# Latent attention on one Trainium2 core: the order of its pieces from a list scheduler, and score maxima issued singly

## The chip, the core and the metric

The kernel runs on one core of one Trainium2 chip. The metric is the device time of one execution in microseconds (us). The kernel before was run three times: median 1757.98 us, lowest 1755.6, highest 1759.52. The five engines that matter are called here by the names of the profile: PE (TensorE), DVE (VectorE), ACT (ScalarE), POOL (GpSimd) and SP (SyncE, which issues DMAs).

## What is computed

The whole program is a stack of layers on one sequence of 2048 tokens of 128 numbers: a mixture of experts, a windowed attention, the mixture again, the latent block, a state space layer, and the latent block a second time. The change touches only the attention inside the latent block, so it acts twice. Cut to that part, the reference is:

```python
q = (x @ Wq.T).reshape(b, t, N_HEADS, HEAD_DIM).transpose(0, 2, 1, 3)        # 16 heads of 8
latent = layernorm(x @ Wdkv.T, ln_g, ln_b)
k = (latent @ Wuk.T).reshape(b, t, N_HEADS, HEAD_DIM).transpose(0, 2, 1, 3)
v = (latent @ Wuv.T).reshape(b, t, N_HEADS, HEAD_DIM).transpose(0, 2, 1, 3)
q, k = apply_rope(q), apply_rope(k)
scores = jnp.einsum('bhqd,bhkd->bhqk', q, k) / np.sqrt(HEAD_DIM)
scores = jnp.where(causal, scores, -jnp.inf)
attn = jax.nn.softmax(scores, axis=-1)
out = jnp.einsum('bhqk,bhkd->bhqd', attn, v).transpose(0, 2, 1, 3).reshape(b, t, D_MODEL)
return out @ Wo.T
```

After it come a residual sum, a root mean square norm and the top-1 choice among four experts.

## The kernel before, in words

Tokens come in 16 tiles of 128, in four groups g = 0 to 3 of 512 query columns. A **unit** v is one group g with four heads (a quarter of the heads, hq). There are 16 units, in the order g = 0,0,1,1,2,2,3,3 and back 3,3,2,2,1,1,0,0 (list `ORDER`). Since attention is causal, a unit of group g has 4, 8, 12 or 16 key tiles (`TILES_OF`), together 160. Every product of scores is made twice, once to find the row maximum and once, with the maximum already subtracted, to feed the exponential:

- **plain** (L1580 on PE, L1714 on ACT): the unit's queries are transposed into a pair of PSUM banks, and ACT copies them out. Without the maximum in them.
- **max** (L1592 on PE; L1761 and L1766 on DVE): one product of 128 queries with up to 512 keys for one head into one of three PSUM banks, 5 to 7 (`bank_of`), and DVE reduces it to a maximum: TENSOR_REDUCE where the keys need no mask, the custom operation with its READ_ACCUMULATOR where they do. There are 4 such items for each key tile, 640 in a block: 384 of full width without a mask, and 256 masked ones, 64 each of 128, 256, 384 and 512 columns. Items m and m + 1 (m even) use the two row halves of the array.
- **chain** (L1804 to L1807 on POOL): after the unit's last item and one small reduce on DVE (L1772), POOL writes the maximum, split in three bf16 numbers, beside the queries.
- **shift** (L1580, L1714 again): the queries are transposed again, now with the maximum.
- **score** (L1602 on PE, L1709 on ACT): half a key tile (two heads) of transposed scores goes into one of two pairs of banks (0 to 3, `pair_of`), and ACT takes the exponential into one of six buffers in SBUF. There are 320 in a block.
- **cut** (L1826 on POOL): the four key tiles on the diagonal are zeroed above it.
- **weigh** (L1618 on PE): the products with the values, into bank 4, in two halves of 256 columns: (v, j, 0) and (v, j, 1).
- **take**, **out** (L1734 ACT; L1628 PE; L1777, L1779 DVE): the unit's result is copied out, turned and divided. After the last unit of a group **rows**, **project** and **square** (L1657, L1680, L1783, L1738) follow, and for groups 2 and 3 **mean, root, norm, turn, logits** and **place**; place ends in eight indirect DMAs that POOL issues (L545).
- Work that rides along: **query** (L1650, L1717) with **aside** (POOL splits queries of groups 2 and 3, L1509 to L1522, four tiles each), and in the first block alone **power** (64 exponentials on ACT, L1742), a product on POOL (L1819, `times_c`) and **states** (L1688, L1729, and SP's DMAs L1873).

Each engine works through its own queue in order. All queues are written from one list of events, made by `plan(far)`. Before, `plan` gives each piece a place on a number line counted in max items: maxima at their own number, scores of unit v spread evenly from nine items (`LEAD`) after its last maximum to nine after the last maximum of unit v + 1, and the rest at fixed offsets; sorting gives the order. PE's waits around the maxima are these:

```python
def bank_free(event):
    if B or number[event] >= 3:
        pe.wait_ge(a_max_got, dve_base + number[event] - 2)
...
if m % 2 == 0:
    bank_free(("max", (v, m + 1)))
```

So before, the even item of a pair waits for the bank of the odd one too, and the odd one waits for nothing.

Of the kernel before, what the change touches and what calls it, by code (L numbers as in the profile page):

```python
# [12 lines left out]
P = 128  # L13
# [12 lines left out]
GT = 4  # L26
NG = NT // GT
GW = GT * P
# [49 lines left out]
def build(nc, ins, out, upto=6):  # L78
    with ExitStack() as ctx:
# [1088 lines left out]
        UNITS, LEAD, N_PROB = len(ORDER), 9, 6  # L1168
# [6 lines left out]
        ITEMS_TO = [4 * n for n in TILES_TO]  # L1175
        N_ITEMS = ITEMS_TO[UNITS]

        def plan(far):

            places = []  # L1180
            start = [ITEMS_TO[v + 1] + LEAD for v in range(UNITS)] + [N_ITEMS + LEAD + 4 * TILES_OF[-1]]
            half_at = [start[v] + (start[v + 1] - start[v]) * s / (2 * TILES_OF[v]) for v in range(UNITS) for s in range(2 * TILES_OF[v])]
            half_at += [half_at[-1] + 2 * k for k in range(1, 24)]
            for v in range(UNITS):
                places += [(ITEMS_TO[v] + m - m % 2, "max", (v, m)) for m in range(4 * TILES_OF[v])]
                places += [(ITEMS_TO[v] - 8 if v else -1, "plain", v), (start[v] - 3.1, "shift", v)]
                places += [(half_at[2 * (TILES_TO[v] + j) + a] - 0.4, "score", (v, j, a)) for j in range(TILES_OF[v]) for a in range(2)]
                for j in range(TILES_OF[v]):
                    step = 2 * (TILES_TO[v] + j) + (4 if j == 0 else 3)
                    if j:  # L1190
                        places += [(half_at[step] + 0.6, "weigh", (v, j, 0))]
                    places += [(half_at[step + (0 < j < TILES_OF[v] - 1)] + 0.6, "weigh", (v, j, 1))]
                places += [(ITEMS_TO[v + 1] + 0.4, "chain", v)]
                places += [(half_at[2 * (TILES_TO[v] + j) + a] + 1.4, "cut", (v, j, a)) for j in range(GT) for a in range(2)]
                places += [(half_at[2 * (TILES_TO[v] + GT) - 1] + 1.5, "aside", v)]
                after = half_at[2 * TILES_TO[v + 1]:]
                places += [(after[2] - 0.2, "take", v), (after[4] - 0.2, "out", v)]
                if v in LAST.values():
# [17 lines left out]
        def tile_of(v, j):  # L1216

            g = ORDER[v][0]
            return GT * g + j if j < GT else j - GT

        def cut(v, j):

            return P * j if j < GT else 0
# [912 lines left out]
```

## Time and profile before

| | |
|---|---|
| median of 3 runs | 1757.98 us |
| the profiled execution's own time | 1757.22 us |
| its span, first to last instruction | 1755.9 us |
| busy in the span: PE, DVE, ACT, POOL | 1238.1, 1196.7, 947.0, 570.0 us |
| latent attention, first block | 492.8 to about 964 us |
| latent attention, second block | 1198 to about 1669 us |
| mean granted clock of TensorE | 0.834 of full speed |

The two attention stages are more than half of the span. A busy share over the whole program says little here; each stretch of a stage has a limit of its own. In the rows, "idle before" is time in which the engine stood still just before the instruction, with what released it behind the arrow; PEld is the loading of weights, which runs beside PE. Records of instructions that follow on one another are merged (x4), and their starts overlap the ends of those before, so the pitch of a run of n is its length, less one overlap, over n.

### The profile page before, as it was taken

What the parts mean: (1) busy time and instruction counts of PE and PEld (TensorE: products, weight loads), DVE (VectorE), ACT (ScalarE), POOL (GpSimd) and SP (SyncE); (2) the same over time, 40 slices, a digit from 0 to 9 for tenths busy, and PEclk for the clock granted to TensorE, in tenths of its full rate; (3) what the DMA queues carried; (4) which work ended last, traced back from release to release, by engine and by line L of the source; (5) the groups of instructions that cost most, each with busy time, mean ns of one, the idle gap of its engine ahead of it and who ended that gap; (6) DMA issues with size and microseconds to landing.
All of it is one profiled execution on the core that took longest, in us unless ns stands there. A gap on an engine that the chain in (4) does not pass through costs nothing. (4 is left out here: it accounts for less than half of the span.)

```text
span 1755.9 us, 36353 instructions
## 1 busy us (share of the span) xinstructions
PE 1238.1 (71%) x13313; PEld 624.7 (36%) x13313; DVE 1196.7 (68%) x3279; ACT 947.0 (54%) x1500; POOL 570.0 (32%) x1032
## 2 busy tenths in 40 slices
PE   2754564366757788899886464776778898988746
PEld 2653453365532122222232453353222222223246
DVE  4358598436777899987862354277789999786234
ACT  0226774122445688888875240134557788887522
POOL 2331276146662411321123242275332111112323
PEclk9977675577577999999998695856799999999869
DMA  9410000021001100000000180000000000000012
GB/s 243 102 46 1 1 4 2 22 66 50 1 18 53 35 1 1 1 2 3 1 1 13 49 217 27 2 1 1 1 1 2 1 2 1 1 2 1 13 44 81
DMA packets 59137, 49.01 MB, mean 28 GB/s; under 512 B 7105, under 2 KB 54194, under 8 KB 58610
## 3 DMA queue, kind: packets, MB, share of 16 engines
q1 hardware_dynamic: 53282, 35.84, 7.9%
q0 software_dynamic: 4736, 9.74, 1.7%
q8 instruction: 109, 1.79, 0.4%
q10 hardware_dynamic: 944, 1.10, 0.2%
q14 instruction: 66, 0.54, 0.1%
HBM read 32.72 MB, written 18.38 MB: 29 GB/s over the span
## 5 line engine op out<-in xcount | busy, mean ns | idle before, releaser
L1709 ACT ACTIVATE arena<-psum 128x1024 f32<-128x1024 f32 (+3 forms) x640 | 561.0, 898 | 191.6 <-PE psum L1602 170.8
L1761 DVE TENSOR_REDUCE arena<-psum 128x1 f32<-128x512 f32 x768 | 479.8, 683 | 63.4 <-PE psum L1592 59.7
L1618 PE MATMUL psum<-arena 128*9 128x256 f32 (+2 forms) x4352 | 346.4, 394 | 0.9 <-POOL arena L1826 0.4
L1592 PE MATMUL psum<-arena 64*128 64x512 bf16 (+3 forms) x1280 | 240.2, 371 | 128.7 <-DVE arena L1761 58.3
L1766 DVE CUSTOM_DVE_ANT_0 arena<-psum,wqkv 128x384 bf16<-128x384 f32 (+3 forms) x512 | 230.3, 486 | 89.0 <-PE psum L1592 75.1
L1602 PE MATMUL psum<-arena 64*128 64x512 bf16 (+3 forms) x1280 | 233.7, 362 | 20.0 <-ACT arena L1709 15.0
L1826 POOL TENSOR_SCALAR_AFFINE_SELECT arena<-arena 128x256 f32<-128x256 f32 x256 | 103.6, 408 | 323.0 <-ACT arena L1709 320.4
L1592 PEld LDWEIGHTS psum<-arena 64*128 64x128 bf16 x1280 | 64.0, 94 | 383.2 <-DVE arena L1761 196.6
L1618 PEld LDWEIGHTS psum<-arena 128*9 128x9 f32 x4352 | 67.7, 89 | 174.3 <-issue 133.5
L1804 POOL CAST arena<-arena 128x16 bf16<-128x16 f32 x64 | 16.4, 257 | 327.7 <-DVE arena L1772 325.4
L677 DVE TENSOR_SCALAR small<-psum,YT 128x128 f32<-128x128 f32 x168 | 50.5, 342 | 78.0 <-PE psum L587 77.4
L632 ACT ACTIVATE small<-psum,YT 128x128 f32<-128x128 f32 x168 | 52.4, 364 | 83.5 <-PE psum L587 64.6
L587 PE MATMUL psum<-arena,YT 128*128 128x128 f32 x672 | 97.1, 292 | 0.1
L1602 PEld LDWEIGHTS psum<-arena 64*128 64x128 bf16 x1280 | 63.5, 95 | 93.1 <-ACT arena L1709 46.6
L1714 ACT ACTIVATE arena<-psum 128x1024 bf16<-128x1024 bf16 x64 | 65.5, 1023 | 52.3 <-PE psum L1580 48.3
L587 PEld LDWEIGHTS psum<-arena,YT 128*128 128x128 f32 x672 | 87.6, 204 | 2.9 <-issue 1.3
L578 PE MATMUL psum<-ident,ACCn 128*128 128x128 f32 x16 | 7.2, 470 | 90.7 <-DMA ACCn<-sorted_rows 58.1
L559 POOL DMA_INDIRECT made_rows<-arena,index x38 | 42.4, 1116 | 76.8 <-DVE arena L657 75.1
L545 POOL DMA_INDIRECT sorted_rows<-Yn,slot x32 | 31.4, 980 | 83.9 <-DVE slot L363 74.8
L597 PE MATMUL psum<-w,small 128*128 x304 | 43.0, 286 | 15.7 <-ACT small L632 12.7
L1580 PE MATMUL psum<-identb,arena 128*128 128x128 bf16 x512 | 44.5, 237 | 9.9 <-DVE psum L1750 3.9
L597 PE MATMUL psum<-big_w,small 128*128 x368 | 50.5, 281 | 0.6 <-issue 0.6
(353 smaller groups left out, 1962.9 us busy)
## 6 DMA issues: line engine op xcount, KB each, us to landing
arena<-taps SPq DMA_DIRECT2D x8, 1024.0 KB
big_w<-in_w SPq DMA_DIRECT2D x2, 2048.0 KB
ACCn<-made_rows SPq DMA_DIRECT2D x16, 256.0 KB, 3.6
regions<-sorted_rows SPq DMA_DIRECT2D x5, 741.8 KB, 4.6
sorted_rows<-arena SPq DMA_DIRECT2D x2, 1483.5 KB, 16.8
ACCn<-regions SPq DMA_DIRECT2D x32, 64.5 KB, 1.9
w<-in_w SPq DMA_DIRECT2D x2, 1024.0 KB
ACCn<-sorted_rows SPq DMA_DIRECT2D x6, 258.0 KB, 3.4
```

The source lines that it names most:

```text
L587: mm = pe.matmul(hidden_of(s, k), first[s % 2][:, k * P:(k + 1) * P], xt[s // GT % 2][:, (s % GT) * P:(s % GT + 1) * P], start=True, stop= ...
L597: mm = pe.matmul(psum[:, 4 + s % 2, 0:D], hid[s % 2][:, k, :], flat2[:, bass.ds(expert[s] * HID + k * P, D)], start=(k == 0), stop=(k == H ...
L632: half = act.activation(hid[s % 2][:, k, :], hidden_of(s, k), ACT.Relu, bias=first[s % 2][:, HID + k:HID + k + 1])
L677: half = dve.tensor_scalar(hid[s % 2][:, k, :], hidden_of(s, k), first[s % 2][:, HID + k:HID + k + 1], 0.0, ALU.add, ALU.max)
L1592: pe.matmul(psum[:, b, 0:w], plain_q[v % 2][rows, a, i * P:(i + 1) * P], keys[rows, 2 * hq + a, c * GW:c * GW + w], start=True, stop=True) ...
L1602: mm = pe.matmul(psum[:, b + r, off:GW], keys[rows, 2 * hq + a, t * P:(t + 1) * P], shift_q[v % 2][rows, a, off:GW], start=True, stop=True)
L1618: mm = pe.matmul(psum[32 * hh:32 * hh + 9, O_BANK, lo:hi], values[:, tile_of(v, j), 4 * hq + hh, :], prob[(t + hh // 2) % N_PROB][:, hh % ...
L1709: act.activation(prob[t % N_PROB][:, :, off:GW], both, ACT.Exp, scale=INV_SQRT_HD).then_inc(a_got, 1)
L1714: act.activation(dst, bank.bitcast(BF16).rearrange("p (a t) -> p a t", a=2), ACT.Copy).then_inc(a_got, 1)
L1761: dve.tensor_reduce(place, bank[:, 0:w], AX.X, ALU.max).then_inc(a_max_got, 1)
L1766: dve.tensor_tensor_reduce(out=masked[cuts % 2][:, 0:w], in0=bank[:, 0:w], in1=causal[:, GW - w:GW], scale=1.0, scalar=LEAST, op0=ALU.add, ...
L1826: pool.affine_select(out=part, in_=part, compare_op=ALU.is_ge, fill=0.0, base=0, pattern=[[0, 2], [1, P]], channel_multiplier=-1).then_inc ...
```

## The change

`plan` is replaced by a list scheduler that runs when the program is built. It keeps a clock for each of PE, DVE, ACT and POOL, a cost for each kind of piece, and the rules of what must be ready (banks, buffers, results), and at each step it emits, of what PE could start soonest, the piece with the best rank: query, plain, shift, small turns, weigh, score, and last a maximum. What it writes down is still one fixed list; nothing is decided on the chip. A maximum is an event of its own place (before, always two together), a unit's weigh halves mostly stand together, the powers go where the model has ACT idle, and POOL's product (`scale`, `times_c`) follows its 16 powers. The costs it believes are in the text: maximum 0.22 us on PE and 0.067 + 0.533 us on DVE at full width, score 0.225 on PE and 1.04 on ACT, weigh 0.225 for each half, chain 1.6, cut 0.42, an aside tile 5.3 on POOL. `place` costs POOL nothing in it, and `states` knows nothing of SP's DMAs. Cut to its core:

```diff
@@ plan @@
-            places = []
-            start = [ITEMS_TO[v + 1] + LEAD for v in range(UNITS)] + [N_ITEMS + LEAD + 4 * TILES_OF[-1]]
...
-                places += [(ITEMS_TO[v] + m - m % 2, "max", (v, m)) for m in range(4 * TILES_OF[v])]
...
+            LAG, events = 0.07, []
+            free = {e: 0.0 for e in ("pe", "dve", "act", "pool")}
...
+                v, m = at["item"]
+                if v < UNITS and ("plain", v) in done:
+                    ready = done["plain", v] + LAG
+                    yield max(ready, ring_free(dve_ring, 3)), 6, "max", (v, m)
+                v, h = at["half"]
+                if v < UNITS and ("shift", v) in done and len(weighed) >= TILES_TO[v] + h // 2 - 2:
+                    yield max(done["shift", v] + LAG, ring_free(act_ring, 2)), 5, "score", (v, h // 2, h % 2)
...
+                options = [(max(free["pe"], ready), *rest) for ready, *rest in choices() if ready < 1e8]
...
+                ready, _, kind, x = min((o for o in options if o[0] <= soonest + 0.05), key=lambda o: o[1])
...
+                    put_dve(kind, x, ready, 0.22 * w / GW, 0.067 + 0.533 * w / GW + (0.085 if c == ORDER[v][0] else 0.0))
...
+                    put_act(kind, x, ready, 0.225 * w / GW, 0.19 + 1.66 * w / 1000)
...
+                    parts = [0.225 * (min(GW, k + GW // 2) - max(k, cut(v, j))) / (GW // 2) for k in (0, GW // 2) if cut(v, j) < k + GW // 2]
+                    for half in ((1,) if j == 0 else (0, 1)):
+                        emit(kind, (v, j, half))
@@ maximum, on PE @@
-                    if m % 2 == 0:
-                        bank_free(("max", (v, m + 1)))
+                    bank_free(event)
@@ attention_pool @@
-                        if far and x in (7, 8):
-                            times_c(2 * x - 14)
-                            times_c(2 * x - 13)
+                    elif kind == "scale":
+                        times_c(x)
```

No product, reduction, exponential or DMA is added or removed. How the order moves is shown at three places.

First, PE in the first block, in the middle of a unit of group 3 (maxima of unit 8 beside scores of unit 7). Before, L1592 is a maximum, L1602 a score, L1618 half a weigh:

```order
L1592 MATMUL psum<-arena 128x512 x2
L1602 MATMUL psum<-arena 128x512 x2
L1618 MATMUL psum<-arena 9x256 x4
L1592 MATMUL psum<-arena 128x512 x2
L1602 MATMUL psum<-arena 128x512 x2
L1618 MATMUL psum<-arena 9x256 x4
L1592 MATMUL psum<-arena 128x512 x2
L1602 MATMUL psum<-arena 128x512 x2
L1618 MATMUL psum<-arena 9x256 x4
```

Now the lines are L1746, L1756 and L1772:

```order
L1756 MATMUL psum<-arena 128x512 x2
L1746 MATMUL psum<-arena 128x512 x2
L1756 MATMUL psum<-arena 128x512 x2
L1746 MATMUL psum<-arena 128x512
L1772 MATMUL psum<-arena 9x256 x8
L1756 MATMUL psum<-arena 128x512 x2
L1746 MATMUL psum<-arena 128x512 x2
L1756 MATMUL psum<-arena 128x512 x2
L1746 MATMUL psum<-arena 128x512
L1772 MATMUL psum<-arena 9x256 x8
```

The two halves of a weigh stand together, once for each key tile, with a score behind them, where they stood apart with two maxima between.

Second, POOL at place, near the end of the first block. Before, L1826 is a cut, L1804 to L1807 a chain, L545 the eight indirect DMAs of place:

```order
L1826 AFFINE_SELECT arena<-arena 128x2x128 x7
L1804 CAST arena<-arena 128x4x4
L1805 TENSOR_TENSOR arena<-arena 128x16
L1804 CAST arena<-arena 128x4x4
L1805 TENSOR_TENSOR arena<-arena 128x16
L1807 CAST arena<-arena 128x4x4
L1826 AFFINE_SELECT arena<-arena 128x2x128
L545 DMA regions<-ACCn,slot 8576x129 x8
L1826 AFFINE_SELECT arena<-arena 128x2x128 x4
```

Now (L1980 is the cut, L1958 to L1961 the chain):

```order
L1980 AFFINE_SELECT arena<-arena 128x2x128
L1958 CAST arena<-arena 128x4x4
L1959 TENSOR_TENSOR arena<-arena 128x16
L1958 CAST arena<-arena 128x4x4
L1959 TENSOR_TENSOR arena<-arena 128x16
L1961 CAST arena<-arena 128x4x4
L545 DMA regions<-ACCn,slot 8576x129 x8
L1980 AFFINE_SELECT arena<-arena 128x2x128 x7
```

All eight cuts of unit 13 now stand behind the DMAs; before, they stood ahead of them. In the list 24 cuts, 32 scores and 7 maxima follow place, where it was 16, 21 and 12, and 27 scores stand behind the last maximum, where it was 13.

Third, PE at a change of units of group 3 (end of the maxima of unit 7, first block), in the change. L1735 is a plain or a shift, L1782 an out:

```order
L1772 MATMUL psum<-arena 9x256 x8
L1746 MATMUL psum<-arena 128x512
L1735 MATMUL psum<-identb,arena 128x128 x8
L1746 MATMUL psum<-arena 128x512 x4
L1782 MATMUL psum<-ident,arena 128x128 x4
L1735 MATMUL psum<-identb,arena 128x128 x8
L1746 MATMUL psum<-arena 128x128 x2
L1746 MATMUL psum<-arena 128x512 x3
L1756 MATMUL psum<-arena 128x512 x4
```

The scores of the old unit end before the new one's begin, and maxima stand alone in between; before, scores stood among them throughout.

## Rows read from the trace of the kernel before

**Rows 1.** Busy time by stretch: us, then PE, PEld, DVE, ACT, POOL, clock, DMA

```profile
495.90:513.00 17.10, 10.43 (x60) 5.61 (x62) 11.08 (x53) 2.81 (x4) 8.65 (x25) 0.50 0.00 0
513.00:600.00 87.00, 66.09 (x574) 19.11 (x570) 71.99 (x194) 48.45 (x63) 32.54 (x92) 0.83 0.16 53
600.00:750.00 150.00, 128.52 (x1372) 33.73 (x1368) 140.05 (x319) 127.62 (x188) 33.42 (x78) 1.00 0.01 2
495.90:943.80 447.90, 373.64 (x3858) 111.24 (x3858) 365.78 (x962) 332.06 (x446) 118.10 (x287) 0.93 0.04 13
1199.00:1650.00 451.00, 374.05 (x3772) 110.28 (x3769) 366.02 (x964) 319.02 (x384) 106.58 (x292) 0.93 0.01 3
```

**Rows 2.** The same view, maxima of units 10 to 15 and the drain

```profile
781.90:818.90 37.00, 35.25 (x476) 12.09 (x472) 27.66 (x67) 31.76 (x38) 4.44 (x13) 1.00 0.02 4
818.90:853.00 34.10, 29.54 (x316) 8.78 (x308) 28.09 (x68) 27.18 (x38) 4.49 (x13) 1.00 0.01 1
900.50:919.10 18.60, 13.77 (x134) 4.84 (x126) 9.97 (x46) 15.76 (x27) 3.68 (x11) 0.91 0.00 1
919.10:943.80 24.70, 19.73 (x176) 6.75 (x176) 9.82 (x46) 14.07 (x18) 11.42 (x19) 0.72 0.07 22
943.80:959.10 15.30, 10.67 (x122) 4.46 (x118) 1.79 (x5) 10.21 (x23) 5.98 (x17) 1.00 0.01 2
```

**Rows 3.** Timeline, DVE: first maximum, the reduce that ends units 5, 8 and 9

```profile
496.24 0.29 DVE L1766 CUSTOM_DVE_ANT_0 arena<-psum,wqkv 128x128 bf16<-128x128 f32 x1 [3.69 <-PE psum L1592]
...
624.56 0.20 DVE L1772 TENSOR_REDUCE arena<-arena 128x16 f32<-128x48 f32 x1
...
742.22 0.22 DVE L1772 TENSOR_REDUCE arena<-arena 128x16 f32<-128x64 f32 x1
781.65 0.22 DVE L1772 TENSOR_REDUCE arena<-arena 128x16 f32<-128x64 f32 x1
```

**Rows 4.** Timeline in full-speed stretches: six maxima on DVE, and PE's pieces

```profile
653.31 3.68 DVE L1761 TENSOR_REDUCE arena<-psum 128x1 f32<-128x512 f32 x6
782.65 0.39 PE L1592 MATMUL psum<-arena 64*128 64x512 bf16 x2 [0.34 <-DVE arena L1761]
782.88 0.38 PE L1602 MATMUL psum<-arena 64*128 64x512 bf16 x2
783.19 0.62 PE L1618 MATMUL psum<-arena 128*9 128x256 f32 x8
658.84 0.62 PE L1618 MATMUL psum<-arena 128*9 128x256 f32 x8
659.40 0.39 PE L1592 MATMUL psum<-arena 64*128 64x512 bf16 x2
907.98 1.05 PE L1618 MATMUL psum<-arena 128*9 128x256 f32 x16
908.96 0.70 PE L1602 MATMUL psum<-arena 64*128 64x384 bf16 x4
894.01 0.62 PE L1580 MATMUL psum<-identb,arena 128*128 128x128 bf16 x8
```

**Rows 5.** Waits on one another in the whole trace: PE's maxima (L1592)

```profile
  DVE arena L1766: 75.1, 100
  DVE arena L1761: 59.7, 121
```

**Rows 6.** Timeline at place: POOL's first and last DMA, and DVE behind them

```profile
927.00 1.09 POOL L545 DMA_INDIRECT regions<-ACCn,slot  x1 [5.12 <-DVE slot L430]
...
935.99 0.95 POOL L545 DMA_INDIRECT regions<-ACCn,slot  x1 [0.31 <-issue]
936.95 0.56 DVE L1766 CUSTOM_DVE_ANT_0 arena<-psum,wqkv 128x384 bf16<-128x384 f32 x1 [6.03 <-remote]
```

**Rows 7.** Timeline, ACT: three scores in a row, and the last take

```profile
895.58 2.85 ACT L1709 ACTIVATE arena<-psum 128x1024 f32<-128x1024 f32 x3
...
958.52 0.60 ACT L1734 ACTIVATE arena<-psum 128x512 f32<-128x512 f32 x1 [1.08 <-PE psum L1618]
```

More of the change, by code:

```diff
@@ L1174, in build @@
         TILES_TO = [sum(TILES_OF[:v]) for v in range(UNITS + 1)]
-        ITEMS_TO = [4 * n for n in TILES_TO]
-        N_ITEMS = ITEMS_TO[UNITS]
-        def plan(far):
-            places = []
-            start = [ITEMS_TO[v + 1] + LEAD for v in range(UNITS)] + [N_ITEMS + LEAD + 4 * TILES_OF[-1]]
-            half_at = [start[v] + (start[v + 1] - start[v]) * s / (2 * TILES_OF[v]) for v in range(UNITS) for s in range(2 * TILES_OF[v])]
-            half_at += [half_at[-1] + 2 * k for k in range(1, 24)]
-            for v in range(UNITS):
-                places += [(ITEMS_TO[v] + m - m % 2, "max", (v, m)) for m in range(4 * TILES_OF[v])]
[L1186 to L1198, printed above, removed]
-                    steps = (6, 10, 14) if ORDER[v][0] >= 2 else (6, 8, 9)
-                    places += [(after[k] - 0.2, name, ORDER[v][0]) for k, name in zip(steps, ("rows", "project", "square"))]
-                if v == LAST[2]:
-                    places += [(after[16 + k] + 0.2, name, 0) for k, name in enumerate(
-                        ("mean", "root", "norm", "", "", "", "", "logits", "", "", "place")) if name]
-                    places += [(after[20 + k] + 0.2, "turn", 2 + k) for k in range(2)]
-            places += [(0.2, "query", 2), (0.3, "aside", -1), (ITEMS_TO[3] + 24.2, "query", 3)]
-            if far:
-                places += [(ITEMS_TO[5] + 4.3 + 3 * a, "power", a) for a in range(64)]
-                places += [(ITEMS_TO[10] + 6.2 + 8 * b, "states", b) for b in range(4)]
-            events = [(kind, x) for _, kind, x in sorted(places, key=lambda p: p[0])]
@@ L1219, in tile_of @@
             return GT * g + j if j < GT else j - GT
-        def cut(v, j):
-            return P * j if j < GT else 0
         N_FILLS = -(-2 * REGION_ROWS // SLOTS)
@@ L1549, in bank_of @@
                 return 5 + number[event] % 3
-            def item(v, m):
-                g = ORDER[v][0]
-                i, a, c, r = m // (4 * (g + 1)), m // (2 * (g + 1)) % 2, m // 2 % (g + 1), m % 2
-                return i, 2 * a + r, c, min(GW, (GT * g + i + 1) * P - c * GW)
             def attention_pe():
@@ L1843, in attention_pool @@
                     elif kind == "aside":
[L1844 to L1850 removed]
+                        g, of = TILES_BESIDE[x]
+                        for i in of:
+                            next_query(g, i)
+                    elif kind == "scale":
+                        times_c(x)
                     elif kind == "place":
```

166 lines of the change are left out of this document (160 added, 6 removed).

## Prediction, written before the changed kernel was run

> **What bounds the kernel now.** I read the busy time by stretch first, since a share over the whole span mixes stages. In the first latent attention DVE works 365.8 us of the 447.9 us between the first maximum and the last, PE 373.6, ACT 332.1; the second attention is the same within 1 us [rows 1]. No engine is full over the stage, so the limit must change on the way, and the rows show three parts. **Start:** until 600 us DVE is busy 83.1 of 104.1 us. **Middle:** from 600 to 750 us DVE is busy 93% of the time, and a unit of group 3 takes 39.4 us (742.2 to 781.7) [rows 3]; six unmasked maxima run in 3.68 us, a pitch of 0.61 to 0.62 us with an overlap at the end [rows 4]. Its work for such a unit is 48 x 0.617 + 16 masked at about 0.41 + 1.0 for the small reduce and an out, or 37.2 us, so DVE is the limit there and 2.2 us of a unit are idle. **End:** from unit 10 on DVE idles much more: 9.3 us of 37.0 in unit 10, 6.0 of 34.1 in unit 11, 8.6 of 18.6 in unit 14 and 14.9 of 24.7 in unit 15 [rows 2]. In unit 10 PE is busy 35.3 of 37.0 us, so there PE is the limit; in units 14 and 15 nobody is, and the time goes in waits. So there are some 82 us of DVE idleness in each block. DVE's waits for maxima of PE make up 134.8 us over both [rows 5], which is nearly all of it. This is what the change can win back; no DVE work goes away.
>
> **What separate waits do.** Before, an even maximum waits until DVE has finished the item two places ahead of it, so when PE is let go DVE holds one item, 0.617 us of work, and a pair needs 0.39 us until its result is there [rows 4]. With semaphores (0.08 us) that leaves PE 0.15 us for anything else. Now item k waits only for k - 3: DVE holds two, 1.23 us, and PE may be 1.23 - 0.39 - 0.08 = 0.76 us late before DVE stands still. The price is that the two items of a pair are let go 0.617 us apart and seldom run side by side: a pair takes 0.23 us from its start to the next piece (782.65 to 782.88), a single one of full width about as long. That is up to 320 x 0.2, less for narrow ones, or some 55 us of PE in each block if they never met; when PE is late both banks are free and they meet again, so it costs least where PE is short. The Trainium skill, TensorE: Matmul & The Clock Gate, section on packing small matmuls, speaks against the change here: products in different row groups overlap, and a pack spans one product plus a few ns for each further one, so splitting packs should cost PE a product each time. The pair's row agrees with the rule about a pair; no row shows a single one. By the rule alone PE would be full in the last part, which is the third rival below.
>
> **The order in the middle (units 6 to 9).** The scheduler believes half a weigh costs PE 0.225 us. The trace says 0.56 for one half (658.84 to 659.40) and 0.98 for two together (907.98 to 908.96) [rows 4]. It now puts both halves and a score between two maxima, once for each key tile. The gap on PE is 0.22 + 0.98 + 0.27 = about 1.5 us from a maximum to the next. Started at its earliest, item k leaves DVE 1.77 us of work from then; the next result comes after 1.5 + 0.39 us. So DVE idles about 0.15 us in each key tile, 2.4 in a unit: 37.2 + 2.4 = 39.6 us against 39.4. Four units: **+1 us** in each block. Bounds: 37.4 us a unit if the gap is covered (-8), and 49 if only one item is in hand (below). I take the value worked from the pieces. PE has 2.47 us for each tile and needs 2 x 0.27 + 0.98 + 4 x 0.22 = 2.40 even with single items, so it fits. ACT needs 2 x 0.95 [rows 7].
>
> **The start (units 0 to 5).** Before, 128.5 us from the first maximum to the end of unit 5's [rows 3], for about 105 us of DVE work: 23 us idle. PE now does a query and two plains ahead of the first maximum, which comes about 1.3 us later (before, DVE lost that time just behind it). Then 16 items come one by one, each on its own bank, and DVE is fed also at the half clock granted there [rows 1]. What stays is the clumps: several weighs in a row after POOL's aside tiles, a query with a plain, outs, at 1 to 2 us each. I count about 12 us. Gain 23 - 12 - 1.3 = **-10 us** for each block; bounds 0 and -17. The powers cost nothing while DVE is behind: they fill ACT where scores wait anyway. Three states stand within a few maxima of one another, and from the second on ACT waits until SP's DMAs have emptied the buffer, which the model doesn't know. POOL's product waits for nothing here. I put it at under 3 us of DVE, inside the 12.
>
> **The end (unit 10 to the last take).** Before: 781.9 to 959.1 us [rows 2, 7], 177 us; in the second block 175. PE's work in it, by the list: 128 scores (72 full at 0.27, 56 on the diagonal at about 0.17) 29 us; 36 full tiles weighed at 0.98 and 28 cut ones at about 0.61, 52; 192 maxima, 17 as pairs and 34 alone; 11 plains and shifts at 0.56, 6; turns, projections and router about 17. Together 121 to 138, say 130. Four states (4 us) have moved out to the start. ACT's is about 122. Neither order can reach it, as pieces wait for one another. Now to the losses left: the root's table loads and the gap behind them, 3 us as before; the last chain of cut, weigh, take, 6 as before; place; and scattered waits, 8% of the work, 11. Place: POOL issues eight DMAs from 927.0 to 936.9 us, and DVE, PE and ACT stood still 5 to 6 us during them without a cut waiting [rows 6]. All eight cuts of unit 13 now stand behind these DMAs, and PE's first weigh of unit 13 waits in order for the second of them, with maxima and scores behind it. That is some 10 us from the first DMA plus 1 for the cuts, less the pieces that PE still has: 8 us, of which 5 to 6 were there before. Sum 130 + 3 + 6 + 8 + 11 = 158: **-18 us** (second block -17). Bounds: 177 (nothing) and 145 (-32). More scores stand behind the last maximum (27 against 13); with 0.95 us each that tail is 13 us longer, and it is in the 158, since it is work that only changed its place.
>
> **Sum.** First block -10 + 1 - 18 = -27, second -10 + 1 - 17 = -26: -53. The profiled execution took 1757.2 us, its span 1755.9; the median of the runs is 0.8 above it. So 1757.2 - 53 + 0.8 = **1705 us**. Nothing outside the two stages changes; what follows them starts earlier by as much.
>
> **Rivals.** *Well covered:* the gap in the middle hides and PE pairs up again by itself: -17, -7 and -28 in each block, -104, 1654 us. For it: 0.76 us of slack where 0.15 kept DVE at 93%. Against it: the weigh is twice as long as believed. Chance 0.17. *It only moves:* the middle loses in its clumps what start and end win, within 0.2% (3.5 us, about what a measurement can tell from none), or a gain under 10 us. Chance 0.10, half on each side of that line. *Slower, by one mechanism:* in the middle the two-item cover isn't there. Where a score stands between two maxima, the first one late makes DVE hold one item when the clump of two weigh halves and a score begins. Then it idles 0.15 + 0.617 = 0.77 us a tile, a tile takes 3.2 us and a unit 49: +40 for each block, and PE, with single items, has no reserve in the end, so the gain there halves. Sum +40 - 10 - 9 = +21 a block, 1800 us. It decides when a unit of group 3 takes more than 46 us. Against it: the list has two maxima on both sides of most clumps, and ACT's buffers let scores wait. Chance 0.14. That the change doesn't do what it says I leave out: the listing of the order shows both parts.
>
> **Numbers.** Forecast 0.59 (its own range 1675 to 1735), well covered 0.17, only moves 0.10, slower 0.14. Faster by over 0.2%: 0.59 + 0.17 + 0.05 = 0.81; the same 0.05; slower 0.14. For 8 in 10, the range reaches over the well covered case (1654) and the small gains, 1650 to 1748.
>
> **What would show it.** Right: DVE busy in the stretch of maxima 366 us as before, but over about 425 us instead of 448; last reduce of unit 5 about 114 us after the first maximum of the block, instead of 128; units of group 3 at 39 to 40 us; from the last reduce of unit 9 to the last take about 158 us; a stop of PE of some 8 us at a weigh behind the eight DMAs. Wrong: units of group 3 above 42 us, or DVE idle before maxima that grows over 135 us in total; or a tail behind the last maximum that eats the start's gain.

## The result, and the profile after

The changed kernel takes **1818.63 us** (median of 4 runs, 1817.31 to 1819.97) against 1758.75 of the kernel before on the same chip: 1.0344 times, 95% interval 1.0326 to 1.0361. It is slower by 60 us, where 1705 was predicted. Its profiled execution has a span of 1816.0 us.

The busy times of the first block, by the same kind of stretches as [rows 1, 2]: units 0 to 3, units 4 and 5, 6 to 9, 10 to 14, 15, and what follows the last maximum up to the last take. Columns are us, PE, PEld, DVE, ACT, POOL, clock, DMA.

```profile
496.30:553.80 57.50, 50.19 (x392) 18.64 (x395) 48.87 (x168) 37.01 (x64) 30.83 (x79) 0.82 0.16 54
553.80:630.80 77.00, 63.70 (x544) 21.60 (x536) 54.67 (x135) 47.91 (x87) 35.13 (x72) 0.80 0.07 21
630.80:810.20 179.40, 153.54 (x1549) 51.55 (x1549) 150.26 (x333) 122.70 (x140) 17.80 (x52) 0.96 0.01 1
810.20:934.20 124.00, 105.52 (x1106) 39.51 (x1109) 101.13 (x282) 97.01 (x129) 19.13 (x57) 1.00 0.01 2
934.20:959.40 25.20, 16.01 (x148) 6.86 (x140) 9.94 (x48) 10.10 (x14) 11.36 (x19) 0.73 0.07 22
959.40:990.20 30.80, 22.18 (x240) 8.14 (x238) 1.85 (x6) 22.77 (x39) 8.33 (x23) 0.94 0.01 1
```

The same stretches of the kernel before:

```profile
496.20:563.60 67.40, 48.45 (x368) 16.96 (x370) 50.54 (x168) 29.52 (x39) 28.07 (x79) 0.71 0.14 46
563.60:624.80 61.20, 48.74 (x492) 13.21 (x493) 54.89 (x136) 42.80 (x61) 23.79 (x66) 0.94 0.08 25
624.80:781.90 157.10, 135.75 (x1444) 34.94 (x1440) 148.03 (x332) 131.74 (x183) 33.23 (x60) 1.00 0.01 1
781.90:919.20 137.30, 120.69 (x1390) 39.22 (x1382) 102.60 (x283) 114.03 (x149) 21.59 (x63) 0.99 0.01 2
```

With 24.6 us for unit 15 and 15.3 behind it ([rows 2] have both within 0.1), the differences are -9.9, +15.8, **+22.3**, -13.3, +0.6 and **+15.5**: +31 us. In the second block the same reading gives -7.4, +7.5, +23.9, -8.9, +1.8, +11.1: +28. Together they are 59 of the 60 us. The gains of the start and of units 10 to 14 are there; units 4 and 5, the middle and the tail take more than they bring. DVE's work is what it was.

Where the reduces stand that answer to [rows 3], on DVE's timeline (first maximum, and the end of units 5, 8 and 9):

```profile
496.29 0.29 DVE L1920 CUSTOM_DVE_ANT_0 arena<-psum,wqkv 128x128 bf16<-128x128 f32 x1 [3.14 <-PE psum L1746]
...
630.60 0.20 DVE L1926 TENSOR_REDUCE arena<-arena 128x16 f32<-128x48 f32 x1
...
765.05 0.22 DVE L1926 TENSOR_REDUCE arena<-arena 128x16 f32<-128x64 f32 x1
810.02 0.22 DVE L1926 TENSOR_REDUCE arena<-arena 128x16 f32<-128x64 f32 x1
```

Unit 9, of group 3, takes 45.0 us (39.4 before). The costliest groups of the page tell who waits now:

```profile
L1915 DVE TENSOR_REDUCE arena<-psum 128x1 f32<-128x512 f32 x768 | 488.0, 685 | 114.7 <-PE psum L1746 113.0
L1746 PE MATMUL psum<-arena 64*128 64x512 bf16 (+3 forms) x1280 | 362.1, 376 | 68.2 <-DVE arena L1915 51.4
L1772 PE MATMUL psum<-arena 128*9 128x256 f32 (+2 forms) x4352 | 315.0, 403 | 56.2 <-ACT arena L1863 36.3
L1920 DVE CUSTOM_DVE_ANT_0 arena<-psum,wqkv 128x384 bf16<-128x384 f32 (+3 forms) x512 | 232.3, 486 | 71.0 <-PE psum L1746 69.2
```

and, of the page of the kernel before:

```profile
L1618 PE MATMUL psum<-arena 128*9 128x256 f32 (+2 forms) x4352 | 346.4, 394 | 0.9 <-POOL arena L1826 0.4
L1592 PE MATMUL psum<-arena 64*128 64x512 bf16 (+3 forms) x1280 | 240.2, 371 | 128.7 <-DVE arena L1761 58.3
```

DVE waits 182.2 us for maxima of PE, where [rows 5] had 134.8. PE waits less for DVE than it did, but a wait has appeared that was not there (0.9 us before): 56.2 us ahead of the weigh products, mostly for exponentials. One tile of the middle shows it, on PE (L1756 score, L1746 maximum, L1772 weigh):

```profile
738.23 0.39 PE L1756 MATMUL psum<-arena 64*128 64x512 bf16 x2
738.46 0.38 PE L1746 MATMUL psum<-arena 64*128 64x512 bf16 x2
738.67 0.38 PE L1756 MATMUL psum<-arena 64*128 64x512 bf16 x2
738.89 0.27 PE L1746 MATMUL psum<-arena 64*128 64x256 bf16 x1
739.74 1.05 PE L1772 MATMUL psum<-arena 128*9 128x256 f32 x16 [0.58 <-ACT arena L1863]
740.72 0.39 PE L1756 MATMUL psum<-arena 64*128 64x512 bf16 x2
...
742.23 1.05 PE L1772 MATMUL psum<-arena 128*9 128x256 f32 x16
```

and on ACT:

```profile
738.66 1.94 ACT L1863 ACTIVATE arena<-psum 128x1024 f32<-128x1024 f32 x2 [0.75 <-PE psum L1756]
741.15 1.94 ACT L1863 ACTIVATE arena<-psum 128x1024 f32<-128x1024 f32 x2 [0.55 <-PE psum L1756]
```

The weigh pair starts at 739.74 and holds PE until 740.72 (0.98). Only then comes the score; its exponential starts 0.43 us later, at 741.15, ends after 0.97, and 0.11 later the next weigh pair starts, at 742.23. That is a **loop of 2.49 us a tile**: no engine in it is full (ACT idles 0.55 of it), but nothing in it can start earlier. The list places about three and a half maxima in a tile of it, where DVE could do four in the time; the rest stand outside the tiles at the change of units, for each unit eight ahead of the first score and five behind the last.

The loop is not the whole of the middle. While DVE takes the maxima of unit 9, PE starts eleven full tiles in 28.3 us (779.54 to 807.88), 2.58 us each in the mean: six of them take 2.49 or 2.50 us, where the next weigh pair waits for the exponential, and five take 2.63 to 2.70, where it stands behind a maximum for which no bank was free. PE's queue runs in order, so such a maximum holds up the weigh pair and the scores behind it too. PE's idle time in the middle (630.8 to 810.2) has both waits at nearly the same size:

```profile
L1746 PE MATMUL psum<-arena 64*128 64x512 bf16 (+3 forms) x257 | 71.0, 372 | 13.0 <-DVE arena L1915 11.8 <-DVE arena L1920 0.5
L1772 PE MATMUL psum<-arena 128*9 128x256 f32 (+2 forms) x928 | 63.8, 388 | 10.8 <-ACT arena L1863 10.5
```

The next section calls the loop T1.

### The profile page after: what moved, and what is told of

It reads as the page before. It is cut to its first block and busy times, and to the rows that moved or that the text cites. A ratio compares the mean times of both kernels' runs of the same rounds, so it can differ in the third digit from the quotient of the medians.

```text
span 1816.0 us, 36349 instructions
## 1 busy us (share of the span) xinstructions
PE 1302.7 (72%) x13313; PEld 695.6 (38%) x13313; DVE 1195.5 (66%) x3279; ACT 936.2 (52%) x1500; POOL 569.7 (31%) x1032
## 5 line engine op out<-in xcount | busy, mean ns | idle before, releaser
L1863 ACT ACTIVATE arena<-psum 128x1024 f32<-128x1024 f32 (+3 forms) x640 | 539.7, 895 | 224.7 <-PE psum L1756 223.9
L1915 DVE TENSOR_REDUCE arena<-psum 128x1 f32<-128x512 f32 x768 | 488.0, 685 | 114.7 <-PE psum L1746 113.0
L1746 PE MATMUL psum<-arena 64*128 64x512 bf16 (+3 forms) x1280 | 362.1, 376 | 68.2 <-DVE arena L1915 51.4
L1772 PE MATMUL psum<-arena 128*9 128x256 f32 (+2 forms) x4352 | 315.0, 403 | 56.2 <-ACT arena L1863 36.3
L1756 PE MATMUL psum<-arena 64*128 64x512 bf16 (+3 forms) x1280 | 239.5, 365 | 19.1 <-ACT arena L1863 14.9
L1746 PEld LDWEIGHTS psum<-arena 64*128 64x128 bf16 x1280 | 100.8, 96 | 257.5 <-DVE arena L1915 147.5
L1980 POOL TENSOR_SCALAR_AFFINE_SELECT arena<-arena 128x256 f32<-128x256 f32 x256 | 102.4, 408 | 279.5 <-ACT arena L1863 276.3
L1772 PEld LDWEIGHTS psum<-arena 128*9 128x9 f32 x4352 | 91.0, 91 | 192.2 <-ACT arena L1863 98.0
L1958 POOL CAST arena<-arena 128x16 bf16<-128x16 f32 x64 | 16.4, 256 | 425.9 <-DVE arena L1926 423.7
L1756 PEld LDWEIGHTS psum<-arena 64*128 64x128 bf16 x1280 | 61.4, 95 | 187.8 <-ACT arena L1863 120.1
L559 POOL DMA_INDIRECT made_rows<-arena,index x38 | 42.5, 1119 | 76.6 <-DVE arena L657 74.9
L545 POOL DMA_INDIRECT sorted_rows<-Yn,slot x32 | 31.3, 978 | 83.9 <-DVE slot L363 74.8
L597 PE MATMUL psum<-w,small 128*128 x304 | 43.2, 287 | 15.4 <-ACT small L632 12.7
L545 POOL DMA_INDIRECT regions<-ACCn,slot x32 | 31.1, 973 | 66.3 <-DVE slot L430 57.8
```

The costliest lines, as they stand in the source:

```text
L545: pool.indirect_dma_start(to, bass.IndirectOffsetOnAxis(slot[:, i:i + 1], 0), rows[:, i, :], None).then_inc(rows_out, 16)
L597: mm = pe.matmul(psum[:, 4 + s % 2, 0:D], hid[s % 2][:, k, :], flat2[:, bass.ds(expert[s] * HID + k * P, D)], start=(k == 0), stop=(k == H ...
L1746: pe.matmul(psum[:, b, 0:w], plain_q[v % 2][rows, a, i * P:(i + 1) * P], keys[rows, 2 * hq + a, c * GW:c * GW + w], start=True, stop=True) ...
L1756: mm = pe.matmul(psum[:, b + r, off:GW], keys[rows, 2 * hq + a, t * P:(t + 1) * P], shift_q[v % 2][rows, a, off:GW], start=True, stop=True)
L1772: mm = pe.matmul(psum[32 * hh:32 * hh + 9, O_BANK, lo:hi], values[:, tile_of(v, j), 4 * hq + hh, :], prob[(t + hh // 2) % N_PROB][:, hh % ...
L1863: act.activation(prob[t % N_PROB][:, :, off:GW], both, ACT.Exp, scale=INV_SQRT_HD).then_inc(a_got, 1)
```

## The experiments

T1 is this loop. T2 is that the scheduler's wrong cost of a weigh alone spoils the order. T3 is that maxima issued singly overfill TensorE, or leave DVE short of an item in hand. All ratios are to the kernel before, run beside each on the same chip (its medians: 1757.1 us for experiments 1 to 4, 1757.0 for 5, 6, 7 and 9, and 1747.6 for 8, 10, 11 and 12, so compare the ratios there; the change itself stands at 1.0344).

**1. The planner's cost alone.**

```diff
-                    parts = [0.225 * (min(GW, ...
+                    parts = [0.49 * (min(GW, ...
```

> The change, with the planner's cost of a half's weigh products at 0.49 us instead of 0.225 (what the pair takes in the trace, 0.98, is now what the plan believes). T1, the loop of weigh, score, exponential and weigh again (0.98 + 0.43 + 0.97 + about 0.11 = 2.49 us a key tile): the list still puts a weigh pair before the score that its exponential frees, so the loop stays; units 6 to 9 of the first block stay at 43 to 46 us each, the time is 1790 to 1820 us. T2, the plan's wrong cost alone: with the right cost the units come to 39 to 40 us, the two stretches of units 6 to 9 lose 40 to 46 us together, and the time is 1755 to 1780 us. T3, that maxima issued one by one overfill TensorE: 1815 to 1825.

Measured: 1857.1 us, 1.0563 (1.0537 to 1.0588). Told the truth about one cost, the scheduler makes a worse order: units 6 to 9 take 47.5 to 48.4 us. T2 falls. T1's range (1790 to 1820) was too low as well: the new list puts both scores of a tile behind the weigh pair, and more maxima outside the tiles at the change of units (17 for unit 8, not 13). PE's waits for exponentials ahead of weighs grow from 10.5 to 16.5 us in the middle of the first block.

**2. Score ahead of weigh.**

```diff
-                    yield ..., 5, "score", (v, h // 2, h % 2)
+                    yield ..., 4, "score", (v, h // 2, h % 2)
-                    yield ready + LAG, 4, "weigh", (v, j)
+                    yield ready + LAG, 5, "weigh", (v, j)
```

> The change, with two ranks of the list scheduler exchanged: a score goes ahead of a weigh pair where both are ready. T1, the loop: the score that an exponential frees is issued ahead of the 0.98 us weigh pair, ScalarE's idle time of 0.55 to 0.75 us a tile ahead of its exponential falls to 0.3 or less, units 6 to 9 of the first block come from 44 to 46 us to 39 to 41, and the time from 1818.6 to 1765 to 1785 us. T2, the plan's wrong weigh cost alone: rank changes little, 1805 to 1825. T3, maxima one by one overfill TensorE: no change, 1810 to 1825.

Measured: 1787.7 us, 1.0171 (1.0137 to 1.0205). Half of the loss is back, by two numbers. ACT now runs four exponentials without a stop:

```profile
748.76 4.14 ACT L1863 ACTIVATE arena<-psum 128x1024 f32<-128x1024 f32 x4 [0.45 <-PE psum L1756]
```

The same stretch of units 6 to 9 (632.0 to 801.4) on PE, in this run:

```profile
L1746 PE MATMUL psum<-arena 64*128 64x512 bf16 (+3 forms) x258 | 73.0, 379 | 13.2 <-DVE arena L1915 12.3
L1772 PE MATMUL psum<-arena 128*9 128x256 f32 (+2 forms) x928 | 64.3, 391 | 0.0
```

The wait of the loop is gone (10.8 us to 0.0), and the middle is shorter by as much: 169.4 us instead of 179.4. The wait for banks ahead of maxima is still there (13.2). So the loop was worth some 10 us of the 22 in the middle of a block. Units 8 and 9 of the second block take 41.0 each, those of the first block 41.0 to 43.3. The full tiles now follow after 1.9 to 2.7 us, 2.28 in the mean, and the same 13 maxima of a unit stand outside the tiles; the 16, and the 1.95 us for every tile, with which the expectation of experiment 6 reckons, are not in the trace. The mechanism was right, and the recovery under T1's range (1765 to 1785).

**3. The pair's wait put back** (the second part of the change undone).

```diff
-                    bank_free(event)
+                    if m % 2 == 0:
+                        bank_free(("max", (v, m + 1)))
```

> The change's order of all pieces, but the rows of a pair of maxima stand behind one wait for both banks, as before the change (its second part undone). T1, the loop: its members are the weigh, the score and the exponential, none of which moves; pairs of rows leave VectorE one item in hand less often, so the time is the same to slower, 1815 to 1830 us. T3, maxima one by one overfill TensorE (their group is busy 362.1 us against 240.2 before): with pairs that share a wait they run side by side again and the time falls by 15 us or more, to under 1804.

Measured: 1925.8 us, 1.0966 (1.0938 to 1.0994). T3 falls in its first form, but T1's number was far off too: the wait costs 107 us in this order. PE in the middle:

```profile
735.07 0.38 PE L1747 MATMUL psum<-arena 64*128 64x512 bf16 x1
736.40 0.39 PE L1747 MATMUL psum<-arena 64*128 64x512 bf16 x1 [0.95 <-DVE arena L1916]
736.71 1.05 PE L1773 MATMUL psum<-arena 128*9 128x256 f32 x16
```

An even maximum waits until only one item is left on DVE, and a 0.98 us weigh pair can stand directly behind it and ahead of its odd partner, as here. PE's wait for DVE's plain reduces ahead of maxima grows from 11.8 to 35.9 us in the middle of the first block. So how many items DVE has in hand matters much in this order, which is what T3's second form says.

**4. The second part alone**, in the old order: the same two lines the other way, in the kernel before.

> The kernel before, with its own order, and only the second part of the change: each maximum's rows wait for their own bank. T1, the loop of the new order is the cause: this part alone costs little or brings a little, 1745 to 1765 us against 1758.75. T3, maxima one by one overfill TensorE: 1770 us or more.

Measured: 1749.15 us, 0.9954 (0.9940 to 0.9969): a small, certain gain.

**5. Half of the weigh work.**

```diff
+                        if j:
+                            hi = (lo + hi) // 2
```

> The change, with half of the value products left out: for every key tile but a unit's first, the weigh products cover only the first half of each half's columns, so the pair takes about 0.5 us instead of 0.98; the order and all other work are the change's. T1, the loop weigh, score, exponential, weigh: it falls from 2.49 to 2.0 us a tile, VectorE is the limit of the middle again, units 6 to 9 of the first block come from 44 to 46 us to 38 to 40.5, and the time from 1818.6 to 1740 to 1770 us. T3, maxima that are short of an item in hand: a stop of 0.8 to 1.0 us a tile stays, the units stay over 43 us, and the time over 1795.

This kernel leaves out half of the value products, so what it returns is not the attention. Measured: 1734.4 us (one run), below T1's range (1740 to 1770). Units 6 to 9 take 39.4, 40.8, 38.8 and 40.0 us. PE in a tile:

```profile
738.96 0.62 PE L1774 MATMUL psum<-arena 128*9 128x128 f32 x16 [0.20 <-ACT arena L1865]
739.52 0.39 PE L1756 MATMUL psum<-arena 64*128 64x512 bf16 x2
...
741.03 0.62 PE L1774 MATMUL psum<-arena 128*9 128x128 f32 x16 [0.45 <-ACT arena L1865]
```

The loop is now 2.07 us, and ACT runs five exponentials in a row behind a stop of 0.33. DVE's idle time in the middle of the first block fell from 29.1 to 10.6 us. That T3's second form is wrong doesn't follow, though: the shorter weigh also shortens the stretch for which DVE's items in hand must last. PE's wait ahead of weighs fell from 10.5 to 5.7 us, and its wait for banks ahead of maxima hardly moved (11.8 and 11.2). The run shows that the weigh's length is what the middle can't hide in this order; what parts the loop from the other waits is experiment 2.

**6. Three ranks.** As in 2, and a maximum ahead of a weigh.

```diff
-                    yield max(ready, ring_free(dve_ring, 3)), 6, "max", (v, m)
+                    yield max(ready, ring_free(dve_ring, 3)), 4.5, "max", (v, m)
```

> The change, with three ranks of the list scheduler altered and nothing else: a score first (4), then a maximum (4.5), then a weigh pair (5). With the score ahead of the weigh alone the time was 1787.7 us, and the list then held three maxima a tile, so ScalarE went through 16 tiles at 1.95 us and 16 maxima stood alone at the end of the unit (16 times 1.95 and 16 times 0.617 make 41). T1 in its second form, a middle needs four maxima a tile and a score ahead of the weigh: the maxima spread, units 6 to 9 come from 41.0 to 43.3 us to 39 to 40.5, the time is 1755 to 1775 us. Rival, the clock granted to TensorE after thin stretches and single maxima that fill it: the units stay at 41 or more, 1780 to 1795.

Measured: **1740.5 us**, 0.9906 (0.9890 to 0.9923), faster than the kernel before and better than T1's range. The stretches of the first block, units 4 and 5, 6 to 9, 10 to 14:

```profile
553.40:618.70 65.30, 55.17 (x525) 19.42 (x517) 54.93 (x134) 46.03 (x87) 35.04 (x72) 0.90 0.08 25
618.70:784.40 165.70, 155.59 (x1567) 50.73 (x1564) 150.34 (x333) 124.01 (x141) 17.71 (x52) 0.95 0.01 2
784.40:894.10 109.70, 103.46 (x1077) 37.94 (x1076) 99.23 (x272) 91.40 (x123) 18.94 (x57) 0.98 0.01 2
```

Against the change each is shorter by 11.7, 13.7 and 14.3 us. The middle itself is still 41.0 to 41.9 us a unit, as the rival said (in the second block 39.9 to 42.4); PE's wait for plain reduces ahead of maxima is down to 4.7 us in it. The surprise is the other stretches, where the same rank had cost as much. So 78 us of the change's time hang on three numbers of a priority list.

**7. The halves apart, and true costs.**

```diff
-                v, j = at["weigh"]
+                v, j, half = at["weigh"]
...
-                    yield max(scaled[at["states"]] + LAG, ring_free(act_ring, 2)), 5, "states", at["states"]
+                    yield max(scaled[at["states"]] + LAG, split[3] + LAG, done.get("unloaded", 0.0), ring_free(act_ring, 2)), 5, "states", at["states"]
...
+                    end = run("pe", ready, 0.49 * max(0, GW // 2 - max(0, cut(v, j) - GW // 2 * half)) / (GW // 2) if j else 0.49 * 2)
...
+                    if kind == "place":
+                        run("pool", free["dve"], 10.1)
```

> The change's scheduler with: ranks maximum 3.5, score 4, weigh 5; the two halves of a weigh pair as two pieces that others may go between; the costs as the trace has them (0.49 us a half, 0.617 us a maximum, 0.98 us an exponential); the states pieces behind the split of the last group's queries and behind their own unloading; POOL kept busy 10.1 us by the placing of tokens. T1: no loop over a whole weigh pair is left and VectorE is fed as in the kernel before, units 6 to 9 at 38.5 to 40 us, and the start and the end are shorter than before; 1705 to 1745 us, below both kernels. Rival, TensorE is full (it is busy 89 per cent of the middle) or its clock falls: 1760 or more.

The ranks are maximum 3.5, score 4, weigh 5; of the edit the pieces and some of the new costs and conditions are shown. Measured: **1723.1 us**, 0.9812 (0.9793 to 0.9832). The middle, units 6 to 9, is level with the kernel before (157.1), and the clock stays at full speed in it, where PE now counts as busy for 154.8 of 156.5 us:

```profile
614.90:771.40 156.50, 154.82 (x1658) 47.59 (x1655) 148.24 (x332) 127.33 (x146) 17.81 (x52) 1.00 0.01 2
887.00:941.50 54.50, 37.60 (x356) 15.75 (x356) 6.34 (x28) 34.69 (x54) 18.67 (x37) 0.81 0.03 11
```

The maxima end 57 us earlier than in the kernel before, the last take only 18: 54.5 us of tail now stand where 15.3 stood.

**8. A pair as one piece again**, all else as in 7.

> The run with halves, with a weigh pair again as one piece (ranks, costs, and the states and placing terms as there). T1, with the pair whole VectorE waits once a tile for 0.98 us of weigh work, though score and maxima rank ahead of it: units 6 to 9 of the first block at 40.5 to 42 us against 39.0 to 39.3, the time 1735 to 1750 us. Rival, the ranks alone do it: as with halves, 1718 to 1728.

Measured: 1742.2 us, 0.9965 (0.9954 to 0.9976); units 42.5, 40.1, 40.1 and 39.4. The time is in T1's range, but no unit is in its 40.5 to 42 us, and three are below it; of the 19 us against experiment 7, 5.6 and 6.0 lie in the two middles. The halves apart are worth 1.2 to 1.5 per cent (the smaller number against experiment 10, on the same chip). The ranks alone don't do it. Nor do the truer costs and the terms for states and place: with a pair whole, experiment 6 is faster without them (0.9906). Which of these terms costs what was not tested one by one.

**9. Ranks by need.** As in 7, with this in place of the fixed ranks. Beside it the weigh, plain, shift and states ranks, the cost of a weigh half (0.45) and the model's delay before ACT (0.2) are new too, and a score may run at most 32 items ahead of the maxima; the run can't tell these apart.

```diff
+ (0.88 if free["dve"] < free["pe"] + 1.20 else 3.51), "max", (v, m)
+ (2.26 if free["act"] < free["pe"] + 0.60 else 6.20), "score", (v, h // 2, h % 2)
```

> The same scheduler as in the run with halves, but a maximum goes first only while VectorE would run dry within 1.2 us of TensorE's time (rank 0.88, else 3.51), a score while ScalarE would within 0.6 us (2.26, else 6.2), and a weigh half last (6.31); a score runs at most 32 items ahead of the maxima's count. T1: both VectorE and ScalarE stay fed; units 6 to 9 at 38.5 to 40 us, the stretch behind the last maximum under 20 us; 1690 to 1735 us, below the run with halves by 5 to 25. Rival, TensorE full or slowed: 1755 or more.

Measured: **1721.6 us**, 0.9805 (0.9788 to 0.9821): no different from 7 within the intervals, where 5 to 25 us less were expected. Its middle takes 157.4 us and its tail is as long (57 us, where under 20 were expected), so the part about the tail fell.

**10. Place later**, all else as in 7.

```diff
-                if ("logits", 0) in done and ("place", 0) not in done:
+                if ("logits", 0) in done and ("place", 0) not in done and at["weigh"][0] >= 14:
```

> The run with halves and one more condition: the placing of tokens is not chosen before the weigh products of unit 13 are all issued. In the run with halves the maxima of the first block ended at 886.8 us and the last take only at 941.5, with TensorE waiting 7.7 and 7.9 us behind POOL. Theory, POOL's transfers hold up the zeroing of exponentials and so TensorE: 3 to 10 us a block come back, 1705 to 1718 us. Rival, the rest of the tail (chain, shift, scores of two small units, clock at half) is what bounds it: 1718 to 1728, no change.

Measured: 1723.0 us, 0.9847 (0.9816 to 0.9879), no gain, as the rival said. In the first block it is 437.6 us from the end of unit 0's maxima to the end of the last take, and 438.0 in the run with halves. What holds the tail up is not settled by this; POOL's transfers alone are not it.

**11. The pair's wait in the order of 6.**

> The order of the run with three ranks altered (score 4, maximum 4.5, weigh 5; 1740.5 us), but the rows of a pair of maxima stand behind one wait for both banks. That order puts the two maxima of a pair often on either side of a score or a weigh pair. Theory, the change's second part is what its first part needs: TensorE's queue stands still until two reduces are done, units 6 to 9 at 45 us or more, 1820 to 1870 us. Rival, the wait matters only in the change's own poor order: 1735 to 1765.

Measured: 1865.7 us, 1.0662 (1.0630 to 1.0695), units 6 to 9 at 43.7 to 47.3 us. Against 1.0 per cent under the kernel before, the pair's wait costs 7.6 per cent here. The wait and the order belong together: an order that parts a pair needs the second part of the change.

**12. States later**, in the change.

```diff
-                    yield max(scaled[at["states"]] + LAG, ring_free(act_ring, 2)), 5, "states", at["states"]
+                    yield max(scaled[at["states"]] + LAG, split[3] + LAG, ring_free(act_ring, 2)), 5, "states", at["states"]
```

> The change, with the states pieces held back until the last group's queries are split. In the change's first block ScalarE and TensorE stood 5.8 and 5.0 us behind POOL for them inside unit 5, which took 43.1 us against 34.8 in the second block, where there are none. Theory: units 4 and 5 of the first block come from 77 to 66 to 70 us, part of it is given back where the states go instead, the time falls by 3 to 8 us to 1811 to 1816. Rival, the place of the states costs the same wherever it is: 1816 to 1821.

Measured: 1816.9 us, 1.0394 (1.0372 to 1.0416): nothing won. The time is the change's within 2 us, but the kernel before ran 11 us faster on this chip, so by the ratio (1.0344 for the change) it may even be 0.5 per cent slower; the two were not run side by side. Units 4 and 5 fell from 77.0 to 68.1 us as expected, but unit 6 rose from 44.5 to 50.2, and from the first small reduce to the last of unit 9 there are 306.9 us where there were 307.0. In the first block the states cost the same in either unit.

## Why the prediction was wrong

**The step that failed is the order in the middle**, "+1 us" a block. It measured the gap on PE between two maxima (1.5 us), and then compared each engine's work with the tile's 2.47 us: PE 2.40, ACT 2 x 0.95, "so it fits". Each does fit. It did not follow the chain that goes round through two engines: the next weigh pair waits for the exponential of a score that stands behind this weigh pair. Read that way, the numbers of [rows 4, 7] (0.98 for the pair, 0.95 for the exponential, 0.39 and some hundredths from a score to ACT) give nearly 2.5 us a tile before any maximum is counted. The change's order, as listed, showed score, weigh, score in that order. Measured: +22.3 and +23.9 us instead of +1. Experiment 2 takes the loop out and wins back 10 us of the first. The rest is of the same step and also a wait in line: the sum looked at what DVE has in hand when a maximum comes late, not at what stands behind a maximum that comes early and finds no bank (11.8 us of PE's idle time). It goes when the maxima get another place in the list: 4.7 us in experiment 6, 0.2 in experiment 7, whose middle is level with the kernel before. One reading was off as well, without weight: by six in 3.68 us the pitch of a full maximum is 0.60 us, not 0.61 to 0.62, so DVE's work in a unit is some 0.8 us less than the 37.2 of the sum.

**The start**, -10 us a block: right for units 0 to 3 (-9.9 and -7.4), with 16 items fed one by one. Units 4 and 5 gave it back (+15.8 and +7.5). I had put the states at under 3 us there; experiment 12 shows that 9 us hang on where they stand in the first block, but also that they can't be had by moving them one unit on. The second block has no states and still lost 7.5 us. The granted clock of these two units is 0.80 in both blocks where it was 0.94, and the ranks of experiment 6 bring 11.7 us back in the first; the cause is not taken apart further.

**The end**, -18 us: from the last reduce of unit 9 to the last take it was 179.9 us instead of 177.2, not 158. The -18 held a gain of about 31 us up to the last maximum, and 13 more behind it for the 27 scores there. The second was near: 15.5 and 11.1 us. The first failed: units 10 to 15 gained 12.7 and 7.1 us. Of the terms, PE's work was put at 130 us, and PE counts as busy for 143.7; the losses were put at 28, and 36.3 are idle. The order of the middle goes on here, since with its three ranks altered (experiment 6) units 10 to 14 take 14.3 us less. Behind the last maximum a full tile costs the whole loop, on PE 2.49 or 2.50 us from one weigh pair to the next, three times:

```profile
965.24 1.05 PE L1772 MATMUL psum<-arena 128*9 128x256 f32 x16 [0.90 <-ACT arena L1863]
966.23 0.60 PE L1756 MATMUL psum<-arena 64*128 64x512 bf16 x4
967.74 1.05 PE L1772 MATMUL psum<-arena 128*9 128x256 f32 x16 [0.90 <-ACT arena L1863]
```

The stop at place was sized right (8 us): the first of POOL's DMAs and PE behind them,

```profile
944.40 1.09 POOL L545 DMA_INDIRECT regions<-ACCn,slot  x1 [8.60 <-DVE slot L430]
```

```profile
955.25 1.89 PE L1772 MATMUL psum<-arena 128*9 128x512 f32 x8 [8.12 <-issue]
```

**The rivals.** The slower one had the right sign, size (1800 for 1818.6) and nearly the place. Its mechanism came in only in part. DVE idles 5.8 us in the eleven full tiles above, 0.52 each (0.61 at the one below) and not 0.77, a unit takes 44.0 to 46.7 us and not 49, and one of eight passed the 46 us at which it was to be decided. Half of PE's waits in the middle are for exponentials, which it didn't have. But that DVE's items in hand carry this order is so: experiment 3 takes one away from each even maximum and costs 107 us. That the sum of this rival came near is partly luck: it had +40 in the middle and -19 outside it, and the first block has +22 and +9. Its chance of 0.14 was too low, because the +1 was held to be worked out when only its throughput was.

```profile
761.84 1.89 DVE L1915 TENSOR_REDUCE arena<-psum 128x1 f32<-128x512 f32 x3 [0.61 <-PE psum L1746]
```

**What would show it**, as the prediction listed: units above 42 us, DVE's waits over 135 us (182), and a tail that eats the start's gain all came in.

**The price of single maxima**, "some 55 us of PE in each block": the busy time of the group of maxima did rise by 121.9 us over both (362.1 against 240.2). But a group's busy time leaves out only overlaps within the group, and a single maximum overlaps with products of other groups. All of PE's busy time rose by 64.6 us (1302.7 against 1238.1), and in experiment 4, where nothing but the wait changes, by 66.8 (1304.9), while the time fell by 0.5 per cent. In the kernel of experiment 7, PE's cycle of two maxima, a score and half a weigh is

```profile
747.89 0.39 PE L1750 MATMUL psum<-arena 64*128 64x512 bf16 x1
747.89 0.60 PE L1760 MATMUL psum<-arena 64*128 64x512 bf16 x2
748.12 0.38 PE L1750 MATMUL psum<-arena 64*128 64x512 bf16 x1
748.42 0.62 PE L1776 MATMUL psum<-arena 128*9 128x256 f32 x8
```

0.53 us for the three, with a maximum and a score's first product started together. In the kernel before, a score and a pair took 0.64 at the place below, but 0.54 at most places, as in [rows 4] from 782.65 to 783.19:

```profile
661.44 0.39 PE L1602 MATMUL psum<-arena 64*128 64x512 bf16 x2
661.76 0.39 PE L1592 MATMUL psum<-arena 64*128 64x512 bf16 x2
662.08 0.62 PE L1618 MATMUL psum<-arena 128*9 128x256 f32 x8
```

So the single maxima cost nothing here, with a product for the other row half next to each, nor do they gain, and the prediction's "by the rule alone PE would be full" drew the wrong case from the rule. The Trainium skill, TensorE: Matmul & The Clock Gate, Part 3 on packing, says that products in different row groups run at once; that holds across a maximum and a score just as within a pair, and the traces agree (747.89 twice).

## What to carry to other kernels

Before an order is judged by each engine's work, take every ring of waits in it and add up the latencies once round: here 0.98 + 0.43 + 0.97 + 0.11 = 2.49 us a tile, and with no engine full. Then look for pieces that are put in the queue before they can run: a maximum without a free bank held up the scores and weighs behind it for as long again as the loop did. In a queue that runs in order, issue first the short piece that another engine waits for, and the long piece that nobody waits for last; a list scheduler needs that in its ranks, and a truer cost without it can make the order worse (1857 us). Splitting the long piece so that others go between was worth another 1.2 to 1.5 per cent here.

## What the hardware showed that I had not expected

**A clock that falls at the change of units.** In the change, behind the end of unit 6 (675.15 us), PE's granted clock drops from 1.00 in the 10 us before, though PE counts as busy:

```profile
673.00:683.00 10.00, 8.36 (x40) 2.86 (x39) 8.62 (x21) 4.69 (x5) 2.24 (x8) 0.64 0.01 2
```

In experiment 7 the same time of the block stays at full speed, with 102 products where there were 40 (its own changes of units, at 654.0 and 693.0, are at full speed too):

```profile
673.00:683.00 10.00, 9.86 (x102) 2.68 (x99) 9.40 (x21) 8.18 (x9) 0.00 (x0) 1.00 0.01 2
```

The change has its lone maxima in that place, one product of 0.22 us for every 0.60 us of DVE. A mean of 0.64 is a stretch spent mostly at 1.2 GHz instead of 2.4. That the lone maxima are what lets the clock fall is argued from this pair of stretches, not shown by a run of its own, and it is not so every time: behind the ends of units 7 and 9 (721.1 and 810.0 us), in the same block and with the same lone maxima, the clock stays at 1.00, and behind unit 8 (765.1) it falls for 3.4 us only. What it costs can be read from the units: unit 8 ran at full clock in both blocks and took 44.0 us, unit 7 at 0.89 and 0.86 and took 45.9 and 46.7. With 44.0 for each of the four, the two middles would be 3.4 and 4.9 us shorter; this is an estimate of the clock's share of the 22 and 24 us.

**A tail that does not shrink.** The last take of the first block ends at 959.1 us in the kernel before and at 941.5, 939.4 and 938.9 in experiments 7, 9 and 10, while the maxima end at 943.8 before and at 887.0, 882.4 and 885.5 there. So of 57 to 61 us won on the maxima 18 to 20 reach the end. Between them lie the chains of the last two units, eight key tiles on the diagonal, place and a clock of 0.81. Which of these sets it is open.
